# VectorE's threshold test of 48 channels, walked channel by channel instead of column by column

## The chip, the cores and the metric

The kernel runs on one core of one Trainium2 chip. The metric is the device time of one execution in microseconds (us). The kernel before took 617.44 us, the median of 3 runs (616.48 to 617.96).

## The reference

The input x is (8, 256, 64, 64) in fp32: 8 images, 256 channels, 64 rows, 64 columns. A layer norm over the channels, a 3x3 mean filter per channel and a residual add give x1. Then each pixel is a token of 256 channels; it is normalised again, and a small "nibble" network works on it:

```
t = t + ffn(ln(t))                                  # t: one token, 256 channels
nibble(base) = argmax(ln(t)[base:base+16] > 0.5)    # base = 16, 32 and 48
mark = ln(t)[0] > 0.5, ln(t)[1] > 0.5, ln(t)[2] > 0.5
```

The three nibbles, two further channels and the marks are the features of a three-layer network of width 80, in an "add" and a "sub" version. Its rounded result sets one of 16 output channels for each of two nibbles, and one carry channel.

## The kernel before

**Layout.** A pair of images fills the 128 partitions (2 x 64 rows). A partition of `xbuf` holds 256 channels x 64 columns in fp32, with the column innermost: neighbouring columns are 4 bytes apart, neighbouring channels 64 words or 256 bytes. There are 4 pairs, and `xbuf` has room for two.

**Staging.** The work goes in chunks of CW = 8 columns, 8 chunks to a pair, 32 in all. Each engine runs 38 steps, and in step t it handles several chunks at different stages: first statistics of chunk t, normalising of chunk t-1, convolution of chunk t-2, decoding of the nibbles of chunk t-3, the network on the chunks before that, and the result of chunk t-6. The order of the instructions of each engine within a step is written out by hand, and semaphores tie the engines together.

**VectorE's step** (lines 590 to 633). Around the change it runs, in this order: the last part of the second statistics' arithmetic (L446 to L456, `sigma`), the comparison with the threshold (`pick(0)`, L503 and L505), three columns of the normalising (`normalise`, L542), statistics of two columns (L552), the weighting of the bits by rank (`pick(1)`, L510), two more columns of L542, an add of the convolution (L570), one more column of L542, the maximum over 16 bits (`pick(2)`, L513), and the rest: L552, L570 and the writing of the result (L488). At the start of a step it waits at L467 for `yt_done`, which TensorE's transposes of L918 signal.

**What depends on it.** L505 writes `g`, a tile of [128, 8 columns, 48 channels] in bf16; a column's 48 channels are contiguous, so neighbouring columns lie 96 bytes apart. L510 reads `g` on the same engine. The semaphore `g_read`, raised by L505, also holds back `low_parts(0)` on GpSimd (L684) and the in-place scaling of `xbuf` on ScalarE (L826, then L771). The three L542 behind L505 raise `n_ready`: ScalarE then rounds half a chunk to fp16 (`nhi`, L816), GpSimd computes the remainder (`nlo`, L650), and TensorE convolves both with a band matrix (L864). GpSimd normalises the fourth column itself (L669) and starts that on `fin_ready`, raised by L456.

Where the threshold is compared, `thr` is a [128, 8] fp32 tile in PSUM and is broadcast over the channels. DMA is issued by SP alone once the weights are in.

Of the kernel before, what the change touches and what calls it, by code (L numbers as in the profile page):

```python
# [9 lines left out]
ALU = mybir.AluOpType  # L10
# [4 lines left out]
P = 128  # L15
# [3 lines left out]
CW = 8  # L19
# [15 lines left out]
ALU_LO, ALU_HI, AX_LO, OP_COL, OUT_LO, OUT_HI, CARRY = 16, 32, 48, 65, 64, 72, 80  # L35
NIB = 16
# [38 lines left out]
class Chain:  # L75
# [13 lines left out]
    def wait(self):  # L89

        wait(self.eng, self.sem, self.base + self.n)
# [47 lines left out]
def build(nc, x_d, wa_d, ba_d, ws_d, bs_d, cst_d, out_d):  # L139
    with ExitStack() as ctx:  # L140
        def sb(name, shape, dt):
            return ctx.enter_context(nc.sbuf_tensor(name, shape, dt))
# [25 lines left out]
        g = sb("g", [P, CW, 3 * NIB], BF16)  # L168
# [42 lines left out]
        def own(n):  # L211

            at = used[0]
            used[0] += n
            assert used[0] <= 512
            return ps[:, B_V, at:at + n]

        eps, r_0, r_n = (own(2 * CW) for _ in range(3))
        thalf, rn, thr, ycar2 = (own(CW) for _ in range(4))
# [43 lines left out]
        def xview(parity):  # L263

            lo = parity * (C * W)
            return xbuf[:, bass.ds(lo, C * W)].rearrange("p (c w) -> p w c", w=W)

        def over(ap, shape):
            return ap.broadcast_to(shape)
# [83 lines left out]
        def _(v):  # L353
# [66 lines left out]
            dvc = Chain(v, g_read, DV_STEPS)  # L420
# [73 lines left out]
            def decode(i, tok, k):  # L494


                c, jc, par = tok
                cols = xview(par)[:, jc * CW:(jc + 1) * CW, :]
                if i == 0:
                    dvc.turn(c)  # L500
                    dvc.wait()
                    wait(v, feat_ready, c - 1)
                    v.tensor_tensor(marks[:, (k + 1) % 2, :, :], cols[:, :, 0:3],  # L503
                                    over(thr.unsqueeze(2), [P, CW, 3]), ALU.is_gt)
                    dvc.count(v.tensor_tensor(g[:, :, :], cols[:, :, ALU_LO:ALU_LO + 3 * NIB],  # L505
                                              over(thr.unsqueeze(2), [P, CW, 3 * NIB]), ALU.is_gt))
                    return
                dvc.wait()
                if i == 1:
                    dvc.count(v.tensor_tensor(gw[:, :, :, :].rearrange("p b k n -> p b (k n)"), g[:, :, :],  # L510
                                              over(rank.unsqueeze(1), [P, CW, 3 * NIB]), ALU.mult))
                else:
                    dvc.count(v.tensor_reduce(mx1[:, (k + 1) % 2, :, :], gw[:, :, :, :], mybir.AxisListType.X,  # L513
                                              ALU.max))
                    dvc.end()

            def step(t, j, pair):
# [60 lines left out]
                def pick(i):  # L578
                    if tok:
                        decode(i, tok, (j - 1) % 4)  # L580
# [394 lines left out]
```

## Time and profile before

| what | value |
|---|---|
| median of the runs | 617.44 us |
| time of the profiled execution | 618.25 us |
| its span, first to last instruction | 616.5 us |
| busy: VectorE, TensorE, ScalarE, GpSimd | 507.8, 479.6, 468.7, 383.9 us |
| mean granted TensorE clock | 0.961 |
| L505, 32 instructions | 26.5 us busy, 829 ns each |

The profiled execution took 1.75 us more than its span and 0.81 us more than the median of the runs. The page gives busy time by engine; the views after it say by line what an engine spent, what it waited for, and which work lies on the chain that ended last. "Mean ns" is the length of one instruction from its start to its end; two instructions of VectorE in a row overlap a little, so the engine's rows add up to somewhat more than the time they take.

### The profile page before, as it was taken

To read this page: it belongs to the slowest core of one execution; us is meant where nothing else is said; L and a number is where in the kernel's file an instruction comes from. 1 tells how busy PE (TensorE), PEld (TensorE's weight loads), DVE (VectorE), ACT (ScalarE), POOL (GpSimd) and SP (SyncE) were. 2 spreads that over 40 slices of the span, in tenths; PEclk is the share of its full clock that TensorE was granted. 3 is DMA by queue.
4 is the path that set the end of the run, shared out by engine and by line. 5 is a ranking of instruction groups with operands and counts; after the bars stand their busy time and mean duration, and the time that the engine had idled before them with its cause. 6 is when DMAs were issued, how large, how long until landed. Compare 5 with 4: busy or idle time off the path is not lost.

```text
span 616.5 us, 8862 instructions
## 1 busy us (share of the span) xinstructions
PE 479.6 (78%) x2294; PEld 201.1 (33%) x2294; DVE 507.8 (82%) x1476; ACT 468.7 (76%) x675; POOL 383.9 (62%) x676
## 2 busy tenths in 40 slices
PE   0035369999989988988899999988999999997750
PEld 0012123333333434333333333433333333433220
DVE  1378979999999999999999999999999999874130
ACT  0011569888888888899999888888888888998730
POOL 0044767777777777777777777777777777764000
PEclk9997779999999999999999999999999999998885
DMA  9999990099877995699559958960598099898998
GB/s 168 191 193 199 193 164 2 0 109 170 133 104 104 171 172 68 103 166 190 80 78 176 173 89 110 137 70 1 68 115 92 1 103 69 64 75 62 88 87 72
DMA packets 592746, 67.97 MB, mean 110 GB/s; under 512 B 592568, under 2 KB 592696, under 8 KB 592696
## 3 DMA queue, kind: packets, MB, share of 16 engines
q1 hardware_dynamic: 591696, 67.30, 88.5%
q8 instruction: 19, 0.31, 0.2%
q14 instruction: 31, 0.25, 0.1%
q10 hardware_dynamic: 1000, 0.11, 0.1%
HBM read 33.84 MB, written 33.55 MB: 109 GB/s over the span
## 4 chain that ended last, share of the span: by engine, by line
DVE 33%; PE 32%; POOL 12%; ACT 11%; issue 5%; SPq 3%; DMA 1%; DVEq 0%; POOLq 0%; ACTq 0%
PE ps L864 13%; PE ps L895 10%; POOL nlo L650 10%; DVE n L542 9%; DVE stat L552 7%; ACT nhi L816 5%; PE ps L918 4%; DVE g L505 4%; DVE xbuf L570 3%; ACT xbuf L771 3%; SPq L287 3%; PE ps L887 2%; DVE ps L481 2%; ACT h L791 1%; PE ps L900 1%
## 5 line engine op out<-in xcount | busy, mean ns | idle before, releaser
L771 ACT ACTIVATE xbuf<-xbuf,shift,gain 128x256 f32<-128x256 f32 x224 | 200.4, 944 | 0.0
L552 DVE BATCH_NORM_STATS2 stat<-xbuf 128x6 f32<-128x512 f32 x256 | 171.2, 685 | 22.0 <-DMA xbuf<-x 21.8
L650 POOL TENSOR_TENSOR nlo<-n,nhi 128x1024 f16<-128x1024 f32 x64 | 137.5, 2149 | 7.5 <-ACT nhi L816 7.4
L895 PE MATMUL ps<-h,w2m 128*128 128x512 f32 x256 | 134.3, 607 | 3.7 <-ACT h L791 2.4
L864 PE MATMUL ps<-nhi,band 128*128 128x512 f16 (+1 forms) x408 | 108.4, 380 | 25.1 <-POOL nlo L650 25.1
L669 POOL TENSOR_SCALAR n<-xbuf,stat,rns 128x256 f32<-128x256 f32 x64 | 94.2, 1478 | 41.4 <-DVE ps L456 41.0
L542 DVE SCALAR_TENSOR_TENSOR n<-xbuf,stat,ps 128x256 f32<-128x256 f32 x192 | 118.8, 663 | 0.1
L864 PE MATMUL ps<-nlo,band 128*128 128x512 f16 (+1 forms) x408 | 107.4, 377 | 0.0
L570 DVE TENSOR_TENSOR xbuf<-ps,xbuf 128x512 f32<-128x512 f32 x128 | 91.5, 715 | 15.6 <-PE ps L864 15.5
L816 ACT ACTIVATE nhi<-n 128x1024 f16<-128x1024 f32 x64 | 67.5, 1054 | 46.6 <-DVE n L542 46.6
L791 ACT ACTIVATE h<-ps,b2m 128x512 f32<-128x512 f32 x128 | 88.0, 687 | 11.4 <-PE ps L895 11.3
L783 ACT ACTIVATE h<-ps 128x512 f32<-128x512 f32 x128 | 75.7, 591 | 19.5 <-PE ps L887 19.5
L659 POOL TENSOR_TENSOR ut<-xbuf,stat 128x16 f32<-128x16 f32 x32 | 7.4, 230 | 123.8 <-DVE ps L456 123.8
L864 PEld LDWEIGHTS ps<-nhi,band 128*128 128x128 f16 x408 | 35.6, 100 | 110.9 <-issue 55.2
L887 PE MATMUL ps<-featT,w 128*128 128x512 bf16 x128 | 49.7, 388 | 28.4 <-ACT featT L808 26.4
L864 PEld LDWEIGHTS ps<-nlo,band 128*128 128x128 f16 x408 | 41.0, 100 | 45.5 <-issue 5.5
L895 PEld LDWEIGHTS ps<-h,w2m 128*128 128x128 f32 x256 | 45.6, 191 | 25.0 <-issue 17.6
L467 DVE SCALAR_TENSOR_TENSOR ps<-ps,msk 128x16 f32<-128x16 f32 x32 | 5.8, 183 | 47.9 <-PE ps L918 47.9
L723 POOL TENSOR_TENSOR feat<-val,msk 128x264 bf16<-128x264 bf16 x64 | 39.1, 635 | 0.2
L918 PEld LDWEIGHTS ps<-consts,ysb 128*128 128x128 f32 x256 | 33.5, 192 | 16.4 <-ACT ysb L821 9.0
L912 PE MATMUL ps<-h2r,w3r 128*128 128x512 f32 x64 | 36.0, 645 | 0.0
L900 PE MATMUL ps<-h,w2r 128*32 128x512 f32 x256 | 35.8, 633 | 0.0
(90 smaller groups left out, 560.0 us busy)
## 6 DMA issues: line engine op xcount, KB each, us to landing
xbuf<-x SPq DMA_DIRECT2D x32, 512.0 KB, 6.9
xbuf<-x SPq DMA_DIRECT2D x16, 1024.0 KB, 11.1
out<-xbuf SPq DMA_DIRECT2D x32, 512.0 KB, 7.4
out<-xbuf SPq DMA_DIRECT2D x12, 1024.0 KB, 12.6
out<-xbuf SPq DMA_DIRECT2D x16, 256.0 KB, 8.3
consts<-cst SPq DMA_DIRECT2D x1, 176.0 KB, 2.4
h<-ws ACTq DMA_DIRECT2D x4, 0.2 KB
b2r<-bs ACTq DMA_DIRECT2D x4, 0.1 KB
```

The lines of the kernel that those rows point to most:

```text
L542: ins = v.scalar_tensor_tensor(n32[:, w // HALF, w % HALF, :], xview(par)[:, jc * CW + w, :], mean[:, k, w:w + 1], over(rn[:, w:w + 1], [P ...
L552: return v.bn_stats(stat[:, j % 4, at + 2 * s:at + 2 * s + 2, :].rearrange("p w n -> p (w n)"), xview(par)[:, w:w + 2, :].rearrange("p w c ...
L570: v.tensor_tensor(pair_cols, ps[:, B_CONV + s % 2, :].rearrange("p (w c) -> p c w", w=2), pair_cols, ALU.add).then_inc(x1_done, 1)
L650: pool.tensor_tensor(nlo[:, at:at + HALF, :], n32[:, h, :, :], nhi[:, at:at + HALF, :], ALU.subtract).then_inc(lo_ready, 1)
L669: pool.tensor_scalar(n32[:, h, HALF - 1, :], xview(par)[:, jc * CW + w, :], mean[:, k, w:w + 1], rns[:, j % 2, w:w + 1], ALU.subtract, ALU ...
L771: ins = act.activation(col, col, ACT.Identity, bias=shift[:, k, w:w + 1], scale=gain[:, k, w:w + 1])
L783: act.activation(h1[:, slot(i, jc), :], ps[:, B_L1, :], ACT.Relu).then_inc(h1_ready, 1)
L791: act.activation(h2[:, slot(i, jc), :], ps[:, B_L2, :], ACT.Relu, bias=b2m[:, 0:1]).then_inc(h2_ready, 1)
L816: act.activation(nhi[:, at:at + HALF, :], n32[:, s - 1, :, :], ACT.Copy).then_inc(hi_ready, 1)
L864: ins = pe.matmul(bank[:, i:i + k, :], band[:, :], src[:, at:at + k, :], start=n == 1, stop=n == 2 * len(pieces))
L887: pe.matmul(ps[:, B_L1, :], w1[:, i % 2, :], featT[:, jc % 2, i // 2, :], start=True, stop=True).then_inc(l1_done, 1)
L895: pe.matmul(ps[:, B_L2, :], w2m[:, :], h1[:, slot(i, jc), :], start=True, stop=True).then_inc(l2_done, 1)
```

## The change

The comparison of L505 gets the same operands with their last two dimensions exchanged. It computes the same 8 x 48 values and puts them at the same addresses of `g`; only the order changes in which the elements are read and written. Before, the inner loop ran over 48 channels and the outer one over 8 columns. After, the inner loop runs over 8 columns and the outer one over 48 channels. L503, L510, L513 and all semaphores stay as they are.

```diff
                     v.tensor_tensor(marks[:, (k + 1) % 2, :, :], cols[:, :, 0:3],
                                     over(thr.unsqueeze(2), [P, CW, 3]), ALU.is_gt)
-                    dvc.count(v.tensor_tensor(g[:, :, :], cols[:, :, ALU_LO:ALU_LO + 3 * NIB],
-                                              over(thr.unsqueeze(2), [P, CW, 3 * NIB]), ALU.is_gt))
+                    dvc.count(v.tensor_tensor(g[:, :, :].rearrange("p b n -> p n b"),
+                                              cols[:, :, ALU_LO:ALU_LO + 3 * NIB].rearrange("p b n -> p n b"),
+                                              over(thr.unsqueeze(1), [P, 3 * NIB, CW]), ALU.is_gt))
                     return
```

| operand of L505 | before: inner step, run | after: inner step, run |
|---|---|---|
| source `xbuf`, fp32 | 256 bytes, 48 long | 4 bytes, 8 long, then a hop of 256 bytes |
| threshold `thr`, fp32 in PSUM | 0 (one value, 48 times) | 4 bytes, 8 long, repeated 48 times |
| destination `g`, bf16 | 2 bytes, 384 in one run | 96 bytes, 8 long |

## Rows read from the trace of the kernel before

**Rows 1.** The page, part 1: busy us, share of the span, instructions.

```profile
PE 479.6 (78%) x2294; PEld 201.1 (33%) x2294; DVE 507.8 (82%) x1476; ACT 468.7 (76%) x675; POOL 383.9 (62%) x676
```

**Rows 2.** Busy time by stretch: `us, PE, PEld, DVE, ACT, POOL, PEclk, DMA, GB/s`.

```profile
130.00:190.00 60.00, 54.58 (x265) 22.65 (x264) 57.53 (x154) 53.99 (x78) 46.91 (x83) 1.00 1.04 139
```

**Rows 3.** Waits from 113 to 530 us: total, times, longest.

```profile
DVE ps L467 <- PE ps L918: 18.6, 25, 0.8
...
POOL nlo L650 <- ACT nhi L816: 5.8, 25, 0.3
```

**Rows 4.** The chain of waits in one step: start, us, what.

```profile
307.93 0.81 DVE g L505
308.74 1.76 DVE n L542 x3
...
310.52 1.06 ACT nhi L816
...
311.72 2.16 POOL nlo L650
...
314.01 1.46 PE ps L864 x6
...
320.14 0.18 DVE ps L467
...
324.07 0.80 DVE g L505
```

**Rows 5.** The chain of waits, first and last L505 on it (26 in all).

```profile
64.23 0.79 DVE g L505
...
533.72 0.80 DVE g L505
```

**Rows 6.** Timeline of VectorE where the chain does not name L505.

```profile
291.79 0.79 DVE L505 TENSOR_TENSOR g<-xbuf,ps 128x384 bf16<-128x384 f32 x1
...
178.35 0.85 DVE L505 TENSOR_TENSOR g<-xbuf,ps 128x384 bf16<-128x384 f32 x1
179.12 1.86 DVE L542 SCALAR_TENSOR_TENSOR n<-xbuf,stat,ps 128x256 f32<-128x256 f32 x3
```

**Rows 7.** VectorE by line, shape: count, busy us, mean ns, idle us.

```profile
L552 DVE BATCH_NORM_STATS2 stat<-xbuf 128x6 f32<-128x512 f32 x256 | 171.2, 685 | 22.0 <-DMA xbuf<-x 21.8
L542 DVE SCALAR_TENSOR_TENSOR n<-xbuf,stat,ps 128x256 f32<-128x256 f32 x192 | 118.8, 663 | 0.1
L570 DVE TENSOR_TENSOR xbuf<-ps,xbuf 128x512 f32<-128x512 f32 x128 | 91.5, 715 | 15.6 <-PE ps L864 15.5
L505 DVE TENSOR_TENSOR g<-xbuf,ps 128x384 bf16<-128x384 f32 x32 | 26.5, 829 | 0.0
L488 DVE SCALAR_TENSOR_TENSOR xbuf<-ps,xbuf 128x128 f32<-128x128 f32 x64 | 24.6, 384 | 0.3
...
L510 DVE TENSOR_TENSOR gw<-g,ps 128x384 bf16<-128x384 bf16 x32 | 17.3, 539 | 0.0
...
L444 DVE TENSOR_TENSOR s_nu<-s_nt,ps 128x16 f32<-128x16 f32 x34 | 5.8, 170 | 0.2
```

**Rows 8.** ScalarE by line and shape, the same columns.

```profile
L771 ACT ACTIVATE xbuf<-xbuf,shift,gain 128x256 f32<-128x256 f32 x224 | 200.4, 944 | 0.0
...
L816 ACT ACTIVATE nhi<-n 128x1024 f16<-128x1024 f32 x64 | 67.5, 1054 | 46.6 <-DVE n L542 46.6
...
L800 ACT ACTIVATE s_sqrt<-s_var 128x16 f32<-128x16 f32 x34 | 7.9, 231 | 20.9 <-DVE s_var L428 20.9
```

**Rows 9.** Timeline of POOL in two steps.

```profile
311.25 0.22 POOL L680 TENSOR_TENSOR val<-ut,rstd 128x16 bf16<-128x16 f32 x1
311.71 2.15 POOL L650 TENSOR_TENSOR nlo<-n,nhi 128x1024 f16<-128x1024 f32 x1 [0.25 <-ACT nhi L816]
...
181.87 0.22 POOL L680 TENSOR_TENSOR val<-ut,rstd 128x16 bf16<-128x16 f32 x1
182.21 2.16 POOL L650 TENSOR_TENSOR nlo<-n,nhi 128x1024 f16<-128x1024 f32 x1
```

## The prediction

> **What bounds the kernel now.** I read the page's busy times first. No engine is busy all the time, but VectorE leads with 82% and its instructions are the most numerous outside TensorE [rows 1]. The table by stretch then says what the whole span hides: from 130 to 190 us VectorE works 57.53 of 60 us, TensorE has its granted clock at 1.00, the 2.4 GHz level, and the other engines have more room [rows 2]. The list of waits shows that even VectorE has a gap. In 25 steps it waits at L467, 18.6 us in all or 0.74 us a step, for TensorE's transposes of L918 [rows 3]. So the middle of the kernel is bound by a loop through several engines.
>
> The chain of waits gives that loop for one step [rows 4]: L505 from 307.93 us, the three L542 behind it, ScalarE's rounding L816 at 310.52, GpSimd's remainder L650 at 311.72, TensorE's convolution L864 at 314.01, and so to VectorE's L467 at 320.14, behind which VectorE runs without a pause to the next L505, at 324.07. Line 505 stands in that loop once a step. The chain names it 26 times, from 64.23 to 533.72 us [rows 5]. Of the 32 steps six are left. In two of them (291.79 is one) the chain puts "issue" in its place and goes on with the L542 behind it, so it counts too. At 178.35 the chain goes by GpSimd, but VectorE's three L542 end at 180.98, and with L816's 1.06 us they come within 0.1 us of GpSimd's own work, which ends at 182.09 [rows 4, 6, 9]: a tie. The other three, one in the filling of the pipeline and the last two, are off the chain. So a longer L505 counts 29 times, once for each instruction.
>
> **The price of the order of elements.** I need two scales. L444 (16 elements, 170 ns) and L510 (384 elements, 539 ns) read and write in contiguous runs; the line through them rises 369 / 368 = 1.00 ns an element [rows 7]. Against it:
> - L505 reads with a step of 64 words and writes contiguously: 829 ns for 384 elements, 290 ns over L510, or 0.755 ns an element.
> - L542 reads in one run of 256 such steps: 663 against 411 ns, or 0.98 ns an element.
> - L488 reads and writes in runs of 16 such steps: 384 against 282 ns, or 0.80 ns.
> - L552 takes two neighbouring columns and then hops 64 words: 685 against 667 ns, 0.04 ns. L570 reads and writes like that, with a step of 256 words in PSUM at every element: 715 ns, 0.09 ns.
>
> For ScalarE, L800 (16 elements, 231 ns) and L816 (1024, 1054 ns) give 0.816 ns an element, so 427 ns for 256. L771 has 256 elements with a step of 64 words on both sides: 944 ns, 2.02 ns an element over the line [rows 8].
>
> **The change, part by part.**
> 1. *The source* now comes in runs of eight neighbouring words. L552 shows that two are enough to stream almost freely. This removes 0.755 x 384 = 290 ns.
> 2. *The threshold* is read as eight words again and again. It lies in PSUM, and L570's steps there cost next to nothing, so I take 0; up to 0.09 x 384 = 35 ns is the bound above, and nothing speaks for a gain, since one value was as near before.
> 3. *The destination* now steps 96 bytes at every element. No instruction of VectorE in this trace writes with a step of 24 words. From below the step is free (L488 writes at a step of 64 words, and with its reads it pays only 0.80 ns, which is 0.04 more than reading alone). From above it is L771's whole 2.02 ns. I take the part of L771 that is left when a stepped read's 0.755 ns is subtracted: 1.265 ns, or 486 ns. The row is from another engine, but it is the only long run that writes with a step, and its surplus is much more than any of the read rows explain. L488 is nearer by engine, but it writes back what it has just read, with its read stalls there to hide the writes.
>
> The new L505 is 539 + 486 = 1025 ns, 196 ns more than now. It stands ahead of the L542 on the loop, so all 29 count: 29 x 0.196 = 5.7 us. No instruction, wait or transfer is added. What waits for line 505's signal, `g_read`, comes behind the normalising anyway: L650 starts 2.98 us after L505 ends, and ScalarE's L771 stands behind L816 [rows 4]. So the later signal costs nothing of its own; were that cover gone, it would cost the same 0.196 us again. Against the profiled execution, 618.25 us, that makes 623.9; that execution is 0.81 us over the median of the runs, so against the median it is 617.44 + 5.7 = 623.1 us.
>
> The trace puts a read that hops 64 words at 1.76 ns an element in all (1.00 + 0.755). The Trainium skill (Vector Engine (DVE) Microarchitecture Reference, section 5.2, Measured stream behaviour on trn2) has 1.73 ns for a source that hops at every element, full rate for runs of two neighbouring words, and 2.50 ns for a destination alone that steps 24 words, this very distance. By its figures L505 would grow by 0.77 x 384 = 296 ns, an estimate that gives 29 x 0.296 = 8.6 us and 626.0. The trace agrees with the first two figures; no row here shows the third.
>
> **The rivals.**
> - *A stepped write costs what a stepped read costs* (17 in 100). For it: L488 with both at 0.80 ns, L505 with one at 0.755. Against it: L771. The new L505 differs by 0.04 x 384 = 17 ns at most, 0.5 us over 29 steps: 617.4 to 617.9, with the 35 ns of the threshold up to 619. That the order of the dimensions does not reach the chip would look the same; I see no reason for it, since L552 and L570 run as they are written. The same page of the Trainium skill lists 1.71 ns for a destination that hops 4 KiB, which would give this case.
> - *The write is free and only the gain is left: faster* (16 in 100). L505 falls to 539 ns. The loop does not give all of it back, because GpSimd is close behind: at 178.35 it went from the end of L680, 182.09, to L650 in 0.12 us; in the step shown L680 ends at 311.47 and L650 starts at 311.71, so it could start only 0.12 us sooner [rows 9]. That decides from 0.12 us on: 28 x 0.12 = 3.4 us, 614.1 us. If GpSimd's own columns also ran faster next to a shorter L505, the bound is 28 x 0.29 = 8.1 us, 609.3. For this: the write ports are not the read ports, and nothing in VectorE's own rows makes a writer pay. Against it: L771.
> - *The full price of L771* (5 in 100): 1.265 more ns than the 0.755 of now, 486 ns an instruction, 14.1 us, 631.5.
>
> **How the numbers follow.** My forecast, a write step that is clearly dearer than a read step, has 62 in 100. Its own range runs from L542's 0.98 ns (0.225 x 384 = 86 ns, 2.5 us, 619.9) to half-way between 1.265 and 2.02 ns (341 ns, 9.9 us, 627.3). A measurement of this kernel can tell about 0.2%, 1.2 us, from no change. The range for eight in ten is 616.2 to 627.3: it takes in the forecast, the equal price and a quarter of the free write, and leaves out 12 and 5 in 100. Slower by over 0.2%: 0.62 + 0.05 = 0.67. Faster: three quarters of the free write, 0.12. Within 0.2%: 0.17 + 0.04 = 0.21.
>
> **What the changed profile would show.** L505's mean is the test of everything: about 1025 ns if I am right, 829 for the equal price, 539 for the free write. The difference between the starts of one L505 and the next, 16.14 us now [rows 4], would grow by as much as the instruction grows, about 0.2 us. The 0.74 us before L467 should stay, because the wait belongs to the same loop, and so should the 0.25 us of GpSimd before L650 [rows 9]; in the faster case that idle time goes, and L680 becomes what L650 follows. L542, L510, L513 and L552 should keep their means; if L542 or GpSimd's L669 changes by tens of ns, a contention that I priced at nothing is at work. I am wrong if L505 grows and the time does not, for then the loop is not what the chain says, and wrong in the other way if L505 stays under 0.87 us.

## The result and the profile after

The changed kernel takes 644.03 us, the median of 4 runs (641.52 to 645.27), against 617.7 us for the kernel before in the same series. The ratio is 1.0425, with a 95% interval of 1.0386 to 1.0464: slower by 26 us, and above the range of 616.2 to 627.3. The profiled execution took 642.93 us, with a span of 641.2.

The page's busy times, which answer to [rows 1]:

```profile
PE 480.6 (75%) x2294; PEld 201.0 (31%) x2294; DVE 533.1 (83%) x1476; ACT 468.2 (73%) x675; POOL 384.1 (60%) x676
```

VectorE has 25.3 us more than before, and the other engines have the same within 1 us. In the changed kernel the lines behind L505 have moved down by one. VectorE by line and shape, with the columns of [rows 7]:

```profile
L553 DVE BATCH_NORM_STATS2 stat<-xbuf 128x6 f32<-128x512 f32 x256 | 171.2, 685 | 22.0 <-DMA xbuf<-x 21.9
L543 DVE SCALAR_TENSOR_TENSOR n<-xbuf,stat,ps 128x256 f32<-128x256 f32 x192 | 117.8, 656 | 0.1
L571 DVE TENSOR_TENSOR xbuf<-ps,xbuf 128x512 f32<-128x512 f32 x128 | 91.4, 714 | 15.5 <-PE ps L865 15.5
L505 DVE TENSOR_TENSOR g<-xbuf,ps 128x384 bf16<-128x384 f32 x32 | 62.9, 1967 | 0.0
...
L511 DVE TENSOR_TENSOR gw<-g,ps 128x384 bf16<-128x384 bf16 x32 | 17.3, 540 | 0.0
```

One row differs. L505 went from 829 to 1967 ns; L543 (before: L542) is 7 ns shorter and the others shown kept their means within 1 ns. So one line, with its 32 instructions, holds the loss, and there is no contention spread over the others. But 32 x 1.138 us would be 36 us, more than VectorE's increase in busy time, and 29 x 1.138 = 33 us is more than the loss. The timeline of VectorE shows why. First the kernel before, L505 and its successor:

```profile
324.07 0.80 DVE L505 TENSOR_TENSOR g<-xbuf,ps 128x384 bf16<-128x384 f32 x1
324.78 1.83 DVE L542 SCALAR_TENSOR_TENSOR n<-xbuf,stat,ps 128x256 f32<-128x256 f32 x3
```

and the changed kernel, with L467 and the next L505 of its step:

```profile
320.72 1.97 DVE L505 TENSOR_TENSOR g<-xbuf,ps 128x384 bf16<-128x384 f32 x1
322.29 1.83 DVE L543 SCALAR_TENSOR_TENSOR n<-xbuf,stat,ps 128x256 f32<-128x256 f32 x3
...
333.73 0.18 DVE L467 SCALAR_TENSOR_TENSOR ps<-ps,msk 128x16 f32<-128x16 f32 x1 [0.77 <-PE ps L919]
...
337.66 1.97 DVE L505 TENSOR_TENSOR g<-xbuf,ps 128x384 bf16<-128x384 f32 x1
```

In the steps shown the successor starts 0.71 us after L505 starts before the change, and 1.57 us after it. The 0.71 is at the short end of its kind: over the first 31 steps of the kernel before the distance runs from 0.71 to 0.78 us, with a mean of 0.75; after the change it is 1.56 to 1.58, mean 1.57. L505 is recorded as 1.97 us long, so for its last 0.40 us the L543 behind it is already running. What an instruction takes from the loop is the time between two starts, and that grew by 0.82 us.

The step, from one L505 to the next, grew by nearly as much: its median over the 31 steps went from 16.14 to 16.94 us. The span grew by 641.2 - 616.5 = 24.7 us, and the steps say where. In 27 of the 31 the growth is 0.64 to 0.86 us, 21.0 us together. The first two steps, in the filling of the pipeline, took 1.7 us more together. One more, from 302.59 to 320.72, took 2.0 us more; the granted clock was 0.91 in it and 1.00 in the steps beside it, so about 1.2 us of this execution goes with the clock and not with the length of L505.

The chain of waits of the same step, which answers to [rows 4]:

```profile
320.72 1.97 DVE g L505
322.69 1.44 DVE n L543 x3
...
324.15 1.07 ACT nhi L817
...
325.35 2.16 POOL nlo L651
...
327.64 1.46 PE ps L865 x6
...
333.73 0.18 DVE ps L467
...
337.66 1.97 DVE g L505
```

It is the same loop, with L505 longer in it. The chain names L505 in 28 steps and puts "issue" in its place in two more (302.59 and 507.03), so all but the last two instructions count: 30, where the prediction had 29. The waits from 113 to 555 us (total, times, longest) answer to [rows 3]:

```profile
ACT nhi L817 <- DVE n L543: 35.5, 26, 2.0
...
POOL nlo L651 <- ACT nhi L817: 27.2, 26, 1.1
PE ps L865 <- POOL nlo L651: 25.1, 23, 1.7
...
DVE ps L467 <- PE ps L919: 20.3, 26, 1.3
```

VectorE's gap before L467 stayed (20.3 us in 26 steps, 0.78 a step). GpSimd's wait for `nhi` before L651 rose from 5.8 us in 25 steps to 27.2 in 26, from 0.23 to 1.05 us a step: its columns start on L456, ahead of L505, so it gains on VectorE what L505 became longer.

### The profile page after: what moved, and what is told of

The parts are those of the page before. It is cut to its first block, busy times and chain, and to the rows that moved or that the text cites. A ratio compares the mean times of both kernels' runs of the same rounds, so it can differ in the third digit from the quotient of the medians.

```text
span 641.2 us, 8862 instructions
## 1 busy us (share of the span) xinstructions
PE 480.6 (75%) x2294; PEld 201.0 (31%) x2294; DVE 533.1 (83%) x1476; ACT 468.2 (73%) x675; POOL 384.1 (60%) x676
## 4 chain that ended last, share of the span: by engine, by line
DVE 37%; PE 30%; POOL 12%; ACT 10%; issue 5%; SPq 3%; DMA 1%; DVEq 0%; POOLq 0%; ACTq 0%
PE ps L865 13%; POOL nlo L651 10%; PE ps L896 9%; DVE g L505 9%; DVE n L543 7%; DVE stat L553 7%; ACT nhi L817 5%; DVE xbuf L571 4%; PE ps L919 3%; SPq L287 3%; ACT xbuf L772 3%; PE ps L888 2%; DVE ps L481 1%; DMA xbuf<-x 1%; ACT h L792 1%
## 5 line engine op out<-in xcount | busy, mean ns | idle before, releaser
L651 POOL TENSOR_TENSOR nlo<-n,nhi 128x1024 f16<-128x1024 f32 x64 | 137.4, 2147 | 32.2 <-ACT nhi L817 32.2
L543 DVE SCALAR_TENSOR_TENSOR n<-xbuf,stat,ps 128x256 f32<-128x256 f32 x192 | 117.8, 656 | 0.1
L505 DVE TENSOR_TENSOR g<-xbuf,ps 128x384 bf16<-128x384 f32 x32 | 62.9, 1967 | 0.0
L467 DVE SCALAR_TENSOR_TENSOR ps<-ps,msk 128x16 f32<-128x16 f32 x32 | 5.8, 183 | 46.5 <-PE ps L919 46.5
```

The costliest lines, as they stand in the source:

```text
L505: dvc.count(v.tensor_tensor(g[:, :, :].rearrange("p b n -> p n b"), cols[:, :, ALU_LO:ALU_LO + 3 * NIB].rearrange("p b n -> p n b"), over( ...
L543: ins = v.scalar_tensor_tensor(n32[:, w // HALF, w % HALF, :], xview(par)[:, jc * CW + w, :], mean[:, k, w:w + 1], over(rn[:, w:w + 1], [P ...
L651: pool.tensor_tensor(nlo[:, at:at + HALF, :], n32[:, h, :, :], nhi[:, at:at + HALF, :], ALU.subtract).then_inc(lo_ready, 1)
```

## The experiments

Two questions were asked: what in the new L505 costs 1428 ns over a contiguous instruction, and whether its place on the loop explains the time. For the first there were three theories, named in the expectations: A, a two-byte element written alone, not next to the one before it, is dear; B, the distance of 24 words between writes is dear, whatever the type; C, the reading side is dear. Only e1, e4b, e8 and e11 were timed in several runs, the others in one each. The runs of the kernel before in one series lie up to 4.9 us apart, so a single run is read by the length of its instructions and steps, and by its time only where that differs by much more.

### What costs: reading or writing

**e1.** The new order is kept, but `g` is stored channel by channel, so that the writes are contiguous and L511 reads across.

```diff
-        g = sb("g", [P, CW, 3 * NIB], BF16)
+        g = sb("g", [P, 3 * NIB, CW], BF16)
...
-                    dvc.count(v.tensor_tensor(g[:, :, :].rearrange("p b n -> p n b"),
+                    dvc.count(v.tensor_tensor(g[:, :, :],
...
-                    dvc.count(v.tensor_tensor(gw[:, :, :, :].rearrange("p b k n -> p b (k n)"), g[:, :, :],
+                    dvc.count(v.tensor_tensor(gw[:, :, :, :].rearrange("p b k n -> p b (k n)"), g[:, :, :].rearrange("p n b -> p b n"),
```

> The new order of L505 is kept, but g is stored channel by channel, so that L505 writes in one contiguous run; L510 reads g with a step of 16 bytes. After the change L505 took 1967 ns, 1428 ns over the 539 ns of a contiguous instruction of this size. Theory A (a two-byte element written alone, not next to the one before, is what costs) and theory B (a distance of 24 words between writes is what costs, whatever the type) both expect L505 at 540 to 580 ns here. Theory C (the reading side costs: eight-word runs of xbuf, or the threshold read as eight words from PSUM) expects it near 1967. L510 should take 539 to 829 ns, a stepped read's price. Time by A and B: the first half of n is ready 0.29 us sooner, of which GpSimd lets 0.12 through, so about 614 us, or up to 618 where the slower L510 holds back the second half of n.

VectorE by line and shape in e1:

```profile
L511 DVE TENSOR_TENSOR gw<-g,ps 128x384 bf16<-128x384 bf16 x32 | 26.9, 840 | 0.0
...
L505 DVE TENSOR_TENSOR g<-xbuf,ps 128x384 bf16<-128x384 f32 x32 | 17.5, 547 | 0.0
```

L505 took 547 ns. The eight-word runs of `xbuf` and the threshold read as eight words together cost 8 ns over L510's 539. Theory C falls: all but 8 ns of the price is on the write side, 1428 / 384 = 3.72 ns an element. What was saved came back at L511, which reads two-byte elements 16 bytes apart: 840 ns in place of 539. The time was 616.55 against 617.25 us, ratio 0.9989 (0.9977 to 1.0001), no difference that can be told, where a gain of 3 us, to 614, was expected.

**e2.** Whole words at exactly the same distance of 24 words: `g` in fp32, in two halves of 24 channels.

```diff
-        g = sb("g", [P, CW, 3 * NIB], BF16)
+        g = sb("g", [P, 2, CW, 3 * NIB // 2], F32)
...
-                    dvc.count(v.tensor_tensor(g[:, :, :].rearrange("p b n -> p n b"),
-                                              cols[:, :, ALU_LO:ALU_LO + 3 * NIB].rearrange("p b n -> p n b"),
+                    dvc.count(v.tensor_tensor(g[:, :, :, :].rearrange("p h b m -> p h m b"),
+                                              cols[:, :, ALU_LO:ALU_LO + 3 * NIB].rearrange("p b (h m) -> p h m b", h=2),
...
```

The threshold is broadcast to the new shape, and L512 (L510 before) reads `g` in the new layout; these lines are left out.

> The new order is kept and g becomes fp32 in two halves of 24 channels, so that neighbouring columns lie exactly 24 words (96 bytes) apart, as in the changed kernel, but each element is a whole word. Theory A (lone two-byte writes) expects L505 to fall far below 1967 ns, to the price of a stepped write of whole words, 829 to 1125 ns. Theory B (the distance) and theory C (the reading side) expect 1967 ns. Time: by A 618 to 626 us, by B and C about 643.

```profile
L505 DVE TENSOR_TENSOR g<-xbuf,ps 128x384 f32<-128x384 f32 x32 | 34.7, 1084 | 0.0
```

1084 ns: the same order and distance cost 545 ns over the contiguous instruction with four-byte elements and 1428 ns with two-byte ones. The time, one run, was 620.35 against 617.25 us. The Trainium skill (Vector Engine (DVE) Microarchitecture Reference, section 5.2, Measured stream behaviour on trn2) has 2.50 ns an element for a destination that steps 24 words, and this run is near it: over the 154 ns at which the line through L444 and L510 starts, (1084 - 154) / 384 = 2.42 ns. Its table is of four-byte elements and does not cover two-byte ones, which were the case here.

**e3.** Two-byte elements again, the columns of `g` 192 bytes apart.

```diff
-        g = sb("g", [P, CW, 3 * NIB], BF16)
+        g_all = sb("g", [P, CW, 6 * NIB], BF16)
+        g = g_all[:, :, 0:3 * NIB]
```

> The new order and bf16 are kept, and the columns of g are moved apart to 48 words (192 bytes). Theory A (lone two-byte writes) expects L505 to stay at 1967 ns, within some 50 ns. Theory B (the distance of 24 words) expects it to change, most likely down toward 829 to 1100 ns. Theory C (the reading side) expects 1967. Time by A and C about 643 us.

```profile
L506 DVE TENSOR_TENSOR g<-xbuf,ps 128x384 bf16<-128x384 f32 x32 | 66.0, 2062 | 0.0
```

2062 ns and 645.15 us, one run. Theory B falls as the main cause: twice the distance is no help, and costs 95 ns more. What a stepped write costs without lone halves of a word is the 545 ns of e2.

**e10.** Each bf16 in a word of its own, the other half never written, columns 192 bytes apart as in e3.

```diff
-        g = sb("g", [P, CW, 3 * NIB], BF16)
+        g_all = sb("g", [P, CW, 3 * NIB, 2], BF16)
+        g = g_all[:, :, :, 0]
```

> The changed kernel with each bf16 element of g in a four-byte word of its own (the other half is never written), columns 192 bytes apart as in e3. If the price of 3.72 ns comes from writing a part of a word, it stays: L505 at 1967 to 2062 ns. If it comes from two writes to the same word, eight elements apart, it falls to the price of a whole word, about 1084 ns. L510 reads with a step of one word and takes 539 to 829 ns.

```profile
L506 DVE TENSOR_TENSOR g<-xbuf,ps 128x384 bf16<-128x384 f32 x32 | 65.8, 2058 | 0.0
```

2058 ns, as in e3 within 4 ns, and 643.78 us in one run. It is not the return to the same word, eight elements later, that costs. L512 reads these elements, a word apart, in 540 ns, as the contiguous ones.

**e7.** The order of the kernel before, with `g` stored as in e1: lone bf16 writes 16 bytes apart, 48 in a row.

```diff
-                    v.tensor_tensor(g[:, :, :], cols[:, :, ALU_LO:ALU_LO + 3 * NIB],
+                    v.tensor_tensor(g[:, :, :].rearrange("p n b -> p b n"), cols[:, :, ALU_LO:ALU_LO + 3 * NIB],
```

> The order of before is kept (48 channels inside), and g is stored channel by channel, so L505 reads with the 64-word step of before and writes lone bf16 elements 16 bytes apart, 48 in a row. If a lone two-byte write costs 3.72 ns whatever the distance and the length of the run, L505 takes 1967 to 2062 ns, the read step hidden under it. If it needs the run of eight or a distance of 96 bytes and more, it takes about 829 to 1100 ns. L510, which reads 16 bytes apart, takes 840 ns as in e1. Time by the first about 643 us, by the second 617 to 626.

```profile
L505 DVE TENSOR_TENSOR g<-xbuf,ps 128x384 bf16<-128x384 f32 x32 | 60.8, 1901 | 0.0
L510 DVE TENSOR_TENSOR gw<-g,ps 128x384 bf16<-128x384 bf16 x32 | 28.4, 888 | 0.0
```

1901 ns, a little under the expected 1967, with 888 ns for L510 against 840, and 642.27 us in one run. The order in which channels and columns are walked has next to nothing to do with the price: lone two-byte writes took 1901 to 2062 ns at 16, 96 and 192 bytes. The stepped read, which cost 290 ns in the kernel before, adds nothing to be seen here.

**e4.** The new order with two channels innermost, so that each visit to a column writes two neighbouring bf16, one whole word, before it hops 96 bytes.

```diff
...
+                        g[:, :, :].rearrange("p b (m i) -> p m b i", i=2),
+                        cols[:, :, ALU_LO:ALU_LO + 3 * NIB].rearrange("p b (m i) -> p m b i", i=2),
+                        over(thr.unsqueeze(1).unsqueeze(3), [P, 3 * NIB // 2, CW, 2]), ALU.is_gt))
```

> Two channels go innermost, then the eight columns, then the 24 pairs: each column gets two neighbouring bf16, one whole word, before the next word 96 bytes on. The read side hops 64 words at every element, so it alone would give about 829 ns. Theory A expects the two halves of a word to be written together: 829 to 1125 ns. If theory A holds but neighbours are not put together, it is near 1967. Theory B (a price for each hop of 24 words) has half as many hops: 539 + 714 = 1253 ns. Theory C expects near 829, since the reading is again as in the kernel before.

616 ns, under every value that was written down, and 615.28 us in the one run. The next row is of the same kernel, timed below as e4b:

```profile
L505 DVE TENSOR_TENSOR g<-xbuf,ps 128x384 bf16<-128x384 f32 x32 | 19.7, 617 | 0.0
```

Theory A holds for the writes: with two halves next to each other, 1351 ns of the 1428 are gone, although the instruction still hops 192 times from column to column. It has no account of the reads, which I expected at 829 ns.

**e13 and e14.** The pairs of e4 with columns 100 bytes apart. In e13 each pair lies across two words, in e14 it fills one. The lines of L505 are those of e4.

```diff
-        g = sb("g", [P, CW, 3 * NIB], BF16)
+        g_all = sb("g", [P, CW, 3 * NIB + 2], BF16)
+        g = g_all[:, :, 1:3 * NIB + 1]      # e13
+        g = g_all[:, :, 0:3 * NIB]          # e14
```

> The pairs of e4, but g starts one element later (its columns 100 bytes apart), so that the two bf16 of every pair lie next to each other in two different four-byte words. In e4 a pair filled a word and L505 took 616 ns. If a write is cheap only where it fills an aligned word, the price of the lone write comes back here: about 1970 ns, or more. If it is enough that two neighbouring elements are written one after the other, L505 stays at 616 ns, or up to 830 where the odd start costs a little.

> The pairs of e4 with g's columns 100 bytes apart as in e13, but starting at a whole word, so that each pair fills one. It tells whether e13's 1266 ns came from the pairs lying across two words or from the distance of 25 words. If a filled word is all that matters, L505 takes 616 ns as in e4; if the distance did it, 1266 ns.

e13 by line and shape, then the list for line 506 of e14 (min/median/max ns, first and last start):

```profile
L506 DVE TENSOR_TENSOR g<-xbuf,ps 128x384 bf16<-128x384 f32 x32 | 40.5, 1266 | 0.0
```

```profile
L506 DVE TENSOR_TENSOR g<-xbuf,ps x32: 552/560/579, 63.6 to 559.8; 128x384 bf16<-128x384 f32 x32
```

At the same distance the pairs that fill a word take 560 ns and those that lie across two take 1266; the times were 614.91 and 625.27 us, one run each. So it takes two elements that fill one aligned word for the low price; that they are neighbours is not enough. e13 still falls short of the 1970 expected: two neighbouring parts of words are cheaper than two lone ones, and no run here says why.

**e12.** Four channels innermost, 8 bytes a visit.

```diff
-                        g[:, :, :].rearrange("p b (m i) -> p m b i", i=2),
+                        g[:, :, :].rearrange("p b (m i) -> p m b i", i=4),
...
```

> Four channels innermost in place of two: each column gets 8 contiguous bytes of g before the next column, 96 bytes on. The write side should be as cheap as in e4 or cheaper. The read side takes four steps of 64 words in a row instead of two. If in e4 the reads were cheap because only two channels' rows take turns, each with the neighbouring column next, L505 rises above 616 ns here, toward the 829 ns of the long runs; if reads are cheap whenever the same stretch of xbuf comes again soon, it stays at 616 ns or falls to 547.

```profile
L505 DVE TENSOR_TENSOR g<-xbuf,ps 128x384 bf16<-128x384 f32 x32 | 26.6, 832 | 0.0
```

832 ns, near the 829 of the kernel before. The writes hop half as often as in e4 and always fill words, so I put the rise down to the reads: four rows of `xbuf` in turn would then cost what 48 in a row cost, and two in turn almost nothing. No run turned the writes of e12 while keeping its reads, so this is argued and not shown. The time was 618.63 us, one run.

### Where it costs: the place in the step

**e9.** The changed kernel with L503 and L505 behind the first three L543 (L542 in the expectation).

```diff
-                pick(0)
                 for w in range(HALF - 1):
                     normalise(w)
+                pick(0)
```

> The changed kernel with L503 and L505 moved behind the first three L542. If L505's length counts only because it stands ahead of the normalising, most of the loss goes: VectorE has 0.74 us of idle time in each step before L467, and the new L505 holds the engine 0.855 us longer, so 0.11 us a step is left, about 3 us, and the time is 618 to 622 us. If every ns of VectorE counts wherever it stands, it stays at 643 us.

636.56 us, one run: 7 of 26 us came back, which neither theory had. The waits of its steady part:

```profile
ACT xbuf L772 <- DVE g L505: 23.4, 25, 1.0
...
DVE ps L467 <- PE ps L919: 11.5, 24, 0.5
...
POOL nlo L651 <- DVE g L505: 6.4, 24, 0.3
```

The signal `g_read` has become a wait that counts: ScalarE's scaling waits 23.4 us for L505, 0.94 us in each of 25 steps, and GpSimd's L651 6.4 us. VectorE's gap before L467 is down to 11.5 us, 0.48 a step, so only 0.26 of its 0.74 us took in any of the longer L505. The median step is 16.75 us, between the 16.14 of the kernel before and the 16.94 of the changed one. Most of the loss is still there, behind the instruction and in what waits for it; the chain of this run begins only at its end, so which of the waits decides is not shown.

**e8.** The same move in the kernel before.

> The kernel before with L503 and L505 moved behind the first three L542, nothing else. If the loop is as the chain of waits gives it, n is ready 0.8 us sooner in each step, GpSimd's own work lets 0.12 us of that through, and the time falls by about 28 x 0.12 = 3.4 us to 614. If what counts is VectorE's sum of work per step, nothing changes: 617 us.

616.3 against 616.95 us, ratio 0.9988 (0.9976 to 1.0000): 0.7 us where I expected 3.4. Its waits:

```profile
DVE ps L467 <- PE ps L918: 15.6, 26, 1.2
...
ACT xbuf L771 <- POOL u L677: 12.9, 26, 0.5
```

ScalarE's scaling L771 now waits 0.5 us a step for GpSimd's L677, which raises `u_read`. I had named only L680 to L650 as GpSimd's limit; this is another, behind the same work. Both stand behind the two columns that GpSimd normalises itself (L669), and these became longer: 1523 ns in place of 1478, two in a step. That takes 0.09 of the 0.12 us that GpSimd was to let through, and 28 x 0.03 = 0.8 us is about what was gained.

**e15.** The kernel before with one more plain instruction ahead of the normalising in each step.

```diff
                 pick(0)
+                if tok:
+                    v.tensor_tensor(spare[:, :, :], over(cst[:, 0:330].unsqueeze(1), [P, 2, 330]),
+                                    over(cst[:, 0:330].unsqueeze(1), [P, 2, 330]), ALU.is_gt)
```

> The kernel before with one more contiguous VectorE instruction in each of the 32 steps, right behind L505 and ahead of the normalising: 660 fp32 elements read twice from a constant tile and written to a spare tile that nobody reads. By the line through L444 and L510 it takes 139 + 662 = 801 ns and its successor starts some 0.71 us after it. If a place ahead of the normalising is on the loop, each step grows by 0.71 us: 29 x 0.71 = 20.6 us, 638 us. If VectorE's gap of 0.74 us before L467 can take it in, 617 to 618.

The timeline around it:

```profile
321.21 0.85 DVE L506 TENSOR_TENSOR g<-xbuf,ps 128x384 bf16<-128x384 f32 x1
321.97 1.00 DVE L611 TENSOR_TENSOR spare<-consts 128x660 f32<-128x660 f32 x1
322.89 1.78 DVE L543 SCALAR_TENSOR_TENSOR n<-xbuf,stat,ps 128x256 f32<-128x256 f32 x3
```

The instruction took 1.00 us, not 0.80 (the sum in the expectation was off too: the line gives 816 ns for 660 elements), and its successor started 0.92 us after it. By its own rows the rule holds: the median step grew from 16.14 to 17.00 us, 0.86, and the span is 643.8 - 616.5 = 27.3 us longer. Two steps (from 166.51 and 440.24 us) were 1.5 and 1.2 us longer than the others, with a granted clock of 0.91 in them. The one run gave 645.55 against 616.66 us. It loses as much as the change does, with every write contiguous.

**e16.** The same instruction right ahead of L467.

> The same extra instruction, put right ahead of L467, into VectorE's idle time. If the loop of the chain holds, it fills the gap of 0.74 us and costs nothing, 617 to 618 us, and the gap falls to about 0.03 us. If VectorE's sum of work is what counts, it costs what it costs in e15, about 638 us.

643.42 us, one run: not free. Here it took 1213 ns, with 1.16 us to the next start, 0.42 us more than the gap holds. And GpSimd's two L727 (before: L723), which run at that moment, became longer:

```profile
L727 POOL TENSOR_TENSOR feat<-val,msk 128x264 bf16<-128x264 bf16 x64 | 56.0, 898 | 0.2
```

898 ns in place of 635. The mean granted clock was 0.934 against 0.961. Two of its steps side by side (us, busy time of PE, PEld, DVE, ACT and POOL, granted clock, DMA share, GB/s):

```profile
285.79:302.29 16.50, 14.14 (x73) 5.95 (x70) 16.46 (x47) 14.29 (x22) 12.55 (x21) 1.00 1.17 185
302.29:320.24 17.95, 15.71 (x73) 6.72 (x75) 16.56 (x47) 14.93 (x22) 12.53 (x21) 0.90 0.46 58
```

The steps tell the effects apart. The median step is 16.52 us, 0.38 over the kernel before, close to the 0.42 us by which the instruction overfills the gap: some 11 us in all. Nine later steps took 17.90 to 18.19 us, 13.5 us together over that median, and in each of them the granted clock was 0.90 or 0.91, where it was 1.00 in the typical ones read beside them. So the gap took in its 0.74 us here too, and the larger part of the loss goes with the clock; what made it fall is not shown. A shorter instruction with a single SBUF operand followed.

**e17.** 480 elements, the second operand from PSUM (`rank`), at the same place.

> As e16, with an extra instruction that fits the gap and reads only one operand from SBUF, the other from PSUM: 480 elements, 139 + 481 = 620 ns, the next one 0.53 us after it. In e16 the extra instruction was longer than the gap (1.16 us to the next start against 0.74) and GpSimd's two L723 beside it went from 635 to 898 ns each. If the gap before L467 is free time, this one costs nothing, 617 us, the gap falls to about 0.2 us and L723 stays at 635 ns. If VectorE's time counts wherever it is spent, it costs 29 x 0.53 = 15 us, 632.

```profile
L595 DVE TENSOR_TENSOR spare<-consts,ps 128x480 f32<-128x480 f32 x32 | 20.4, 639 | 0.1
```

```profile
319.89 0.64 DVE L595 TENSOR_TENSOR spare<-consts,ps 128x480 f32<-128x480 f32 x1
320.71 0.18 DVE L468 SCALAR_TENSOR_TENSOR ps<-ps,msk 128x16 f32<-128x16 f32 x1 [0.17 <-PE ps L923]
```

The gap before L468 (before: L467) fell from 0.74 to 0.17 us, L723 stayed at 637 ns (here L728), and the median step is 16.15 us against 16.14. The span is 617.0 us, against 616.5 in the profiled execution of the kernel before; the one run gave 618.79 against 616.84, a difference that single runs of one kernel show too. So an instruction of 639 ns in each step costs next to nothing in the gap, where ahead of the normalising the 0.53 us of the expectation would have cost 15. (The line gives 635 ns for 480 elements, not the 620 of the expectation.)

### A version that beats both

**e4b.** The kernel of e4, timed in 12 runs.

> The kernel of e4 again, timed. L505 takes 616 ns, 213 less than before, and the next instruction starts 0.50 us after it in place of 0.72. GpSimd's own work was to let 0.12 us a step through: 3.4 us, 613.8. The one run of e4 gave 2.0 us less than the kernel before, so I expect 614 to 616 us and a ratio of 0.995 to 0.998. If L505 at 616 ns were worth nothing, the ratio would be 1.000.

616.49 us (12 runs) against 617.94 (23 runs), ratio 0.9974 (0.9958 to 0.9990): faster than before, by little. Its chain of waits:

```profile
305.50 3.01 POOL n L671 x2
308.51 0.19 POOL u L679
...
308.73 0.02 ACT xbuf L773
...
321.32 0.62 DVE g L505
```

The step is 16.09 us (from 305.23 to 321.32, in the timeline below), 0.05 less than before, although the successor of L505 starts 0.21 us sooner. The chain names L505 in 5 steps, where it was 26. In the step from 305.23 it goes by GpSimd's two L671 and its L679, which raises `u_read`, and on to ScalarE's scaling L773.

```profile
305.23 0.61 DVE L505 TENSOR_TENSOR g<-xbuf,ps 128x384 bf16<-128x384 f32 x1
305.73 1.89 DVE L544 SCALAR_TENSOR_TENSOR n<-xbuf,stat,ps 128x256 f32<-128x256 f32 x3
...
321.32 0.62 DVE L505 TENSOR_TENSOR g<-xbuf,ps 128x384 bf16<-128x384 f32 x1
```

GpSimd's two columns of the normalising are ahead of everything on that way, and they have become longer. First the kernel before, then e4b:

```profile
L669 POOL TENSOR_SCALAR n<-xbuf,stat,rns 128x256 f32<-128x256 f32 x64 | 94.2, 1478 | 41.4 <-DVE ps L456 41.0 <-issue 0.2
L671 POOL TENSOR_SCALAR n<-xbuf,stat,rns 128x256 f32<-128x256 f32 x64 | 96.7, 1519 | 41.2 <-DVE ps L456 40.8 <-issue 0.2
```

Two of them take 0.08 us more in a step, and 0.12 us was all that GpSimd was to let through. What is left, 0.04 us, is what the median step lost (16.14 to 16.10). Whether `u_read` alone decides is open: in this step L679 ends at 308.70, and ScalarE's own L818, ahead of L773, at 308.72.

**e11.** e4 with L503 and L505 moved as in e8.

> The pairs of e4 with L503 and L505 moved behind the first three L542. With GpSimd the one that holds back L650 in both, moving gives nothing on top of e4: 614 to 616 us. If VectorE's later work (the second half of n, the additions of the convolution) bounds e4, moving changes nothing there either. Should n's first half be worth more than GpSimd's 0.12 us, this version beats e4 by up to 29 x 0.3 us, 8 us.

616.27 us, ratio 0.9977 (0.9958 to 0.9996): nothing on top of e4, as expected with GpSimd the limit.

## Why the prediction was wrong

- **What bounds the kernel** was right. The loop of the chain is the same after the change, L505 counts in 30 steps where 29 were forecast, and e15 and e17 show that time ahead of the normalising counts and time in the gap before L467 does not.
- **The source and the threshold** (parts 1 and 2) were right: 547 ns in e1 against 539, and the bound of 35 ns for the threshold holds.
- **The destination** (part 3) is the step that failed. I priced the write at 486 ns for 384 elements, from ScalarE's L771; it measured 1967 - 539 = 1428 ns, and even the upper bound, all of L771's 2.02 ns an element, was only 776. Every row I had put beside it writes either whole words or contiguously. The property that set the price, two-byte elements that leave a part of a word written alone, was in the table of the operands, and no part of the sum looked at it. As a distance of 24 words alone the write measured 545 ns (e2), near my 486; that is luck, since the 486 came from another engine and another step.
- **The length of the instruction** was a second, smaller fault in the same term: I counted it whole, and expected the step to grow by all of it. With the measured length that would have given 29 x 1.138 = 33 us. The last 0.40 us of L505 overlaps its successor, and the step grew by 0.80 us.
- **The signs in the profile.** That the 0.74 us before L467 would stay was right. That GpSimd's 0.25 us before L650 would stay was wrong, whatever the price: GpSimd's columns start ahead of L505, so its wait had to grow with it, and it grew by 0.82 us a step.
- **The rivals** of equal price and of a free write are excluded by 1967 ns. The faster one was right that GpSimd is close behind, but e8 and e4b show a gain of 0.7 and 1.5 us, not 3.4. GpSimd's L669, which was to keep its length, became 45 and 41 ns longer in them, which the prediction priced at nothing. The sentence that `g_read` is covered held in the changed kernel, where L651 starts 2.66 us after L505 ends, and e9 shows a wait of 0.94 us for it where the cover is gone.

## What to carry to other kernels

Before an access pattern is turned for the sake of its reads, look at what the writes become, by element size as well as by step: the two-byte results here that were written alone took 3.5 to 3.8 times as long as the contiguous 539 ns, and taking two at a time (e4) brought it back to 616. Price an instruction on a loop by the distance between its start and its successor's, and look for the next limit behind the one named, since a gain ends there. Where a kernel's steps repeat, compare their median first and the odd ones after it: single steps with a lower clock can make up a large part of a loss, as in e16.

## What the runs showed of the hardware that was not expected

- A VectorE instruction of 384 elements takes 1901 to 2062 ns when each bf16 is written alone (16, 96 or 192 bytes apart, with the other half of the word written or not), 1084 when each element is a whole word 96 bytes from the last, and 560 to 616 when two bf16 fill a word before each hop.
- The next instruction of VectorE starts before the recorded end of the one before: 0.08 us before it on the mean in the kernel before, and 0.21 (e2), 0.40 (after the change) and 0.42 us (e3, e10) where the writes are what the instruction is slow by.
- Reads that step 64 words took little where two rows take turns and the neighbouring column comes next (616 and 560 ns in all), and much with four rows (832) or 48 (829). That the reads make this difference is argued (e12).
- In five of the kernels with longer steps, single steps in the middle took 1.0 to 1.7 us more than the typical one, each with a granted clock of 0.90 or 0.91 in place of 1.00: one after the change, in e7 and in e9, two in e15, nine in e16. The kernel before had none. No run shows what sets them off.
- GpSimd's column of the normalising and VectorE's L542, which run side by side, both became longer where L505 was shorter or moved behind: 1478 and 663 ns before, 1519 and 674 in e4b, 1523 and 681 in e8.
- An instruction whose two operands both lie in SBUF took 1005 ns for 660 elements, where the line through L444 and L510 gives 816, and beside GpSimd's L723 it took 1213 ns while L723 went from 635 to 898. Whether the two operands or something else about it is the cause wasn't tried.
- The same pairs take 616 ns with columns 96 bytes apart and 560 with 100. No run here explains the 56 ns.
